# Keys by token of blocks 3 to 12: four turns of the activated keys and a product on VectorE, in place of eight turns of the finished keys and two copies on ScalarE

## What is computed

```
k = silu(x @ Wk)                                  # 16 heads of 8
k = concatenate([k * cos(theta*n), k * sin(theta*n)], -1)   # n: the token's number in its sequence
energy = (q @ k.T) * causal_mask                  # per head
out = energy @ v
```

## Time and profile before

| | us |
|---|---|
| median of 3 runs | 818.68 |
| lowest, highest | 814.37, 819.54 |
| the profiled execution, its time | 816.64 |
| its span, first to last instruction | 814.9 |

### The profile page before, as it was taken

How to read it: one execution, slowest core, us unless ns; L and a number is a source line. 1 busy time by engine, 2 the same in 40 slices (tenths; PEclk the granted TensorE clock), 3 DMA queues, 4 the chain that set the end, 5 groups by cost and what they waited for, 6 DMA issues and landing times.

```text
span 814.9 us, 27612 instructions
## 1 busy us (share of the span) xinstructions
PE 764.3 (94%) x10798; PEld 617.1 (76%) x10798; DVE 587.7 (72%) x1865; ACT 378.9 (46%) x826; POOL 441.6 (54%) x446
## 2 busy tenths in 40 slices
PE   5889999999999999999988899889999999999993
PEld 4666777777777777777776666779899998999883
DVE  7487898988889888898887899734544445443684
ACT  6434565746556465564653432223332233333583
POOL 6441344634446354453554665661877777876332
PEclk9999999999999999999999999999999999999998
DMA  4155334253442434434242322122554344443555
GB/s 149 45 177 178 102 93 109 66 125 74 101 104 75 120 77 102 103 77 116 63 113 66 80 68 84 40 72 93 105 99 86 42 96 99 72 56 43 134 139 148
DMA packets 73712, 77.18 MB, mean 95 GB/s; under 512 B 11955, under 2 KB 54762, under 8 KB 73584
## 3 DMA queue, kind: packets, MB, share of 16 engines
q1 hardware_dynamic: 56488, 59.15, 27.2%
q0 software_dynamic: 17024, 16.28, 11.2%
q10 hardware_dynamic: 72, 0.00, 0.0%
HBM read 23.99 MB, written 28.89 MB: 65 GB/s over the span
## 4 chain that ended last, share of the span: by engine, by line
PE 72%; DVE 17%; issue 6%; DMA 2%; POOL 2%; ACT 1%; DVEq 0%; POOLq 0%; ACTq 0%; SPq 0%
PE bank L1958 5%; PE bank L2540 4%; PE energy_and_gate_banks L2540 4%; PE bank L1960 4%; PE bank L1959 4%; PE energy_and_gate_banks L1958 4%; DVE EM L1348 3%; PE energy_banks L1958 3%; PE bank L1999 3%; PE energy_banks L1960 3%; PE energy_banks L1959 3%; PE energy_banks L2054 3%; PE energy_and_gate_banks L1960 3%; PE energy_and_gate_banks L1959 3%; PE energy_and_gate_banks L2090 3%
## 5 line engine op out<-in xcount | busy, mean ns | idle before, releaser
L707 POOL DMA_INDIRECT dispatched_rows<-x,slot x128 | 136.4, 1066 | 195.1 <-PE energy_banks L2054 98.8
L847 POOL DMA_INDIRECT summed_rows<-VP,goal_i x80 | 123.8, 1548 | 42.7 <-issue 22.7
L1224 ACT ACTIVATE sq<-energy_banks 128x512 f32<-128x512 f32 (+1 forms) x96 | 50.5, 527 | 120.2 <-PE energy_banks L1960 116.6
L933 ACT ACTIVATE hidden_rounded<-sf 128x512 fp32r<-128x512 f32 x88 | 55.3, 628 | 60.7 <-DVE sf L1378 60.7
L923 ACT ACTIVATE sf<-energy_and_gate_banks 128x512 f32<-128x512 f32 x88 | 52.4, 596 | 62.8 <-PE energy_and_gate_banks L1960 62.3
L1378 DVE TENSOR_TENSOR sf<-sf,bank 128x512 f32<-128x512 f32 x88 | 60.2, 684 | 15.6 <-PE bank L1960 14.5
L1348 DVE TENSOR_TENSOR EM<-energy_and_gate_banks,causal 128x512 f32<-128x512 f32 x64 | 43.9, 686 | 19.1 <-PE energy_banks L2079 13.1
L1958 PE MATMUL energy_and_gate_banks<-xgT_hi,ws_hi 128*128 128x512 f32 x108 | 51.8, 480 | 4.2 <-DVE EM L1348 2.8
L1958 PE MATMUL bank<-xgT_hi,ws_hi 128*128 128x512 f32 x108 | 46.0, 426 | 3.4 <-DVE sf L1378 1.9
L1830 DVE TENSOR_TENSOR he<-sq,bank 128x512 f32<-128x512 f32 (+1 forms) x48 | 28.7, 599 | 27.1 <-PE bank L1960 22.3
L1348 DVE TENSOR_TENSOR EM<-energy_banks,causal 128x512 f32<-128x512 f32 x64 | 43.4, 678 | 0.0
(11 more groups left out here) (271 smaller groups left out, 2266.0 us busy)
## 6 DMA issues: line engine op xcount, KB each, us to landing
QM<-QT SPq DMA_DIRECT2D x248, 32.0 KB
dispatched_rows<-empty POOLq DMA_DIRECT2D x8, 655.0 KB, 4.9
QM<-dispatched_rows SPq DMA_DIRECT2D x8, 655.0 KB, 6.0
QT<-sq SPq DMA_DIRECT2D x40, 128.0 KB
KT<-sq SPq DMA_DIRECT2D x40, 128.0 KB
VP<-QM SPq DMA_DIRECT2D x20, 256.0 KB
xin<-in_x SPq DMA_DIRECT2D x16, 256.0 KB, 4.0
QM<-summed_rows SPq DMA_DIRECT2D x16, 256.0 KB, 2.8
```

What stands on the lines that cost most here:

```text
L707: g.indirect_dma_start(out=xg_d, out_offset=bass.IndirectOffsetOnAxis(ap=slot[:, n % 2, j:j + 1], axis=0), in_=x1[:, n % 2, j % NC, :], in ...
L847: g.indirect_dma_start(out=sum_d, out_offset=bass.IndirectOffsetOnAxis(ap=goal_i[:, par, t:t + 1], axis=0), in_=ye[:, par, t, :], in_offse ...
L933: a.activation(hs_hi[:, f], sf[:, n % SF], ACT.Copy).then_inc(a_hh, 1)
```

## The change

- `keys_once_turned` on PE, right after `shared_pair(1)`: four 128x128 transposes of `sq[:, 1]`, the 128 activated key features, into PB[1]. `keys_turned` is no longer called in steps 2 to 11.
- `keys_by_token` moves from ACT to DVE, between `mask_state(5)` and `hidden_lo(1)`: two products of 128x512 that read 256 columns of PB[1] each (every element twice) and `table_T`, the angle table with tokens in partitions, and write `Kt`. `values_projected(1)` now waits for them, since it writes PB[1].
- `table_T` is made once: eight transposes of `table` into UB in steps 1 and 2 (`table_turned`, PE, after `input_turned`) and two copies on ACT (`table_by_token`). It lies in `x1t`, which the SP program fills from step 12 on.
- `input_turned` and `turn_x1` wait for the values and the gate (`a_v`, `a_th`), which are the last to read their banks, in place of `a_kt`; POOL's `dispatch` number 6 waits for the energies (`pe_E`) in place of the turned keys; ACT's Silu of the keys waits until the keys of the block before are turned.
- The token numbers are raised by a `tensor_tensor` with a tensor `two_blocks` [128, 4] that holds 1024, in place of the `tensor_scalar` with the number.

The same numbers are computed in both. The diff, cut to its core:

```diff
+        table_T = flat(x1t).rearrange("p (c n) -> p c n", c=NC)
...
# POOL
-                    need(gp, pe_kt, 2 * f + 2)
+                    need(gp, pe_E, 8 * b + 8)
                     dispatch(b - 1, (6,))
...
# ACT
+                    if i == 1 and projected_once(f - 1):
+                        need(act, pe_kt, 2 * f)
...
+                def table_by_token(i):
+                    need(act, pe_tab, i + 1)
+                    a.activation(table_T[:, 2 * i:2 * i + 2], UB[:].rearrange("p (c n) -> p c n", c=2), ACT.Copy).then_inc(a_tab, 1)
...
                     hidden_hi(b, 5)
-                    keys_by_token()
                     shared_silu(b, 6)
...
# DVE
-                v.tensor_scalar(x1[:, buf, :, D], x1[:, buf, :, D], 2.0 * S, None, ALU.add).then_inc(v_tok, 1)
+                if b == 1:
+                    dve.wait_ge(c_two, 1)
+                v.tensor_tensor(x1[:, buf, :, D], x1[:, buf, :, D], two_blocks[:], ALU.add).then_inc(v_tok, 1)
...
+                def keys_by_token():
+                    for i in (0, 1):
+                        need(dve, pe_kt, 2 * f + i + 1)
+                        need(dve, pe_S, NS * (f - 1))
+                        need(dve, a_tab, 2)
+                        by_feature = PB[1][:, 256 * i:256 * i + 256].unsqueeze(2).broadcast_to([P, 256, 2])
+                        v.tensor_tensor(Kt[:, fp, 2 * i:2 * i + 2].rearrange("p c (k t) -> p (c k) t", t=2), by_feature,
+                                        table_T[:, 2 * i:2 * i + 2].rearrange("p c (k t) -> p (c k) t", t=2), ALU.mult).then_inc(a_kt, 1)
...
                     mask_state(b, 5)
+                    keys_by_token()
                     hidden_lo(b, 1)
...
# PE
                 def input_turned(n=f):
-                    if n > 1:
+                    if projected_once(n - 1):
+                        need(pe, a_v, 4 * n - 2)
+                        need(pe, a_th, 2 * n - 1)
+                    elif n > 1:
                         need(pe, a_kt, 2 * n - 1)
...
                 def values_projected(i):
...
+                    if projected_once(f) and i == 1:
+                        need(pe, a_kt, 2 * f + 2)
...
+                def keys_once_turned():
+                    need(pe, a_silu, 4 * f + 4)
+                    need(pe, v_lg, f - 2)
+                    for c in range(NC):
+                        ins = t.transpose(PB[1][:, P * c:P * (c + 1)], sq[:, 1, P * c:P * (c + 1)], ident[:])
+                        if c % 2:
+                            ins.then_inc(pe_kt, 1)
...
                     shared_pair(1)
+                    keys_once_turned()
                     states_and_out(2)
...
                     energies_and_state(3)
-                    keys_turned()
                     positions(b)
```

More of the change, by code:

```diff
@@ L96, in build @@
         table = sb("table", [P, 2, S])
+        two_blocks = sb("two_blocks", [P, NC])
         rwt_s = sb("rwt_s", [P, E])
@@ L205, in build @@
         EB = [EB2[:, 0], EB2[:, 1], GB, UB]
-        ld_w = sem("weights_loaded"); ld_q = sem("wqk_loaded"); ld_g = sem("wv_g1_g2_loaded"); ld_t = sem("theta_loaded"); z_vp = sem("values_cleared"); z_qm = sem("q_by_head_cleared"); ld_x = sem("x_loaded"); c_pool = sem("pool_constants"); c_id = sem("identity")
+        ld_w = sem("weights_loaded"); ld_q = sem("wqk_loaded"); ld_g = sem("wv_g1_g2_loaded"); ld_t = sem("theta_loaded"); z_vp = sem("values_cleared"); z_qm = sem("q_by_head_cleared"); ld_x = sem("x_loaded"); c_pool = sem("pool_constants"); c_id = sem("identity"); c_two = sem("token_step_ready")
         c_dve = sem("dve_constants"); c_sin = sem("table_ready"); c_g = sem("g1g2_product"); a_wq = sem("wqk_hi_ready"); v_wq = sem("wqk_lo_ready"); v_ang = sem("angles_ready"); a_g = sem("g1g2_copied"); a_wvg = sem("wvg_hi_ready"); v_wvg = sem("wvg_lo_ready"); a_bf = sem("before_ready"); c_warm = sem("act_table_warm")
@@ L216, in build @@
         pe_kt = sem("k_by_token")
+        pe_tab = sem("table_turned"); a_tab = sem("table_by_token")
         pe_E = sem("energies")
@@ L484, in step @@
                     need(sp, v_x1, 4 * (b - 1))
+                    need(sp, a_kt, 2 * (DIRECT + 2) + 2)
                     sp.dma_start(sum_b[b - 2].rearrange("p (c d) -> p c d", c=NC), x1[:, par, :, 0:D]).then_inc(sp_x1b, 16)
@@ L641, in _ @@
             g.memset(expert[:], 0.0).then_inc(c_pool, 1)
+            g.memset(two_blocks[:], 2.0 * S).then_inc(c_two, 1)
             gp.wait_ge(ld_q, 16)
@@ L1011, in first_blocks @@
                         copy_out(b - 1, 3, 1 - par)
+                        table_by_token(0)
                     silu(f, fp, 0)
@@ L1046, in with_feed_forward @@
                         silu(f, fp, 0)
+                        table_by_token(1)
                         rows_turned()
@@ L2189, in values_projected, with table_turned @@
                     ins.then_inc(pe_vg, 1)
+                def table_turned(i):
+                    if i == 0:
+                        need(pe, a_xhi, 2)
+                    need(pe, a_tab, i)
+                    for c in (0, 1):
+                        for half in (0, 1):
+                            ins = t.transpose(UB[:, 256 * c + P * half:256 * c + P * half + P],
+                                              table[:, half, P * (2 * i + c):P * (2 * i + c + 1)], ident[:])
+                    ins.then_inc(pe_tab, 1)
+                def keys_once_turned():
[5 more added lines that the diff above has]
+                            ins.then_inc(pe_kt, 1)
                 def keys_turned():
@@ L2220, in first_blocks @@
                         input_turned()
+                        table_turned(0)
                     states_and_out(0)
@@ L2245, in with_feed_forward @@
                         input_turned()
+                        table_turned(1)
                         states_and_out(0)
@@ L2262, in with_feed_forward @@
                     project(f, 1)
+                    if b == 2:
+                        need(pe, a_tab, 2)
                     shared_up(0)
@@ L2372, in turn_x1 @@
                 need(pe, v_x1, 4 * (b - 1))
-                need(pe, a_kt, 2 * last(b) + 2)
+                if projected_once(last(b)):
+                    need(pe, a_v, 4 * last(b) + 4)
+                    need(pe, a_th, 2 * last(b) + 2)
+                else:
+                    need(pe, a_kt, 2 * last(b) + 2)
                 if DIRECT + 2 < b < B - 1:
```

## The result

| | before | after |
|---|---|---|
| median of 10 runs, us | 818.28 | 822.57 |
| lowest, highest | 812.58, 820.01 | 820.22, 827.18 |
| profiled execution: its time, its span | 816.64, 814.9 | 821.94, 820.2 |

The ratio is 1.0073, with a 95% interval of 1.0051 to 1.0094: slower by 0.7%, clear of noise and inside what was called "within 1%". The forecast was 825.0, which is 1.0077 of the 818.68 it started from. By the medians the kernel is 4.3 us slower, by the means of the ten runs (817.11 and 823.16) 6.0.

What follows compares the result with a forecast made beforehand. The prediction took PE and VectorE to bound stretches of each step in turn; only the products counted, 10 x 0.63 = +6.3 us on 818.68, giving 825.0 us. Its own range was 823.5 to 827.5, eight times in ten 817.5 to 829.0.

Steps and rivals of the forecast that it cites:

- What bounds: Chain through a step: PE to about 345 us, VectorE to mask(2), PE to energies 3, VectorE, then PE from 363.27.
- Rival A: PE's spared turns reach the end: 0.46 us less a step, 4.6 us in all, 814.1 us; chance 0.08.
- The turns removed: Eight turns on PE after energies 3, 0.93 us a step, beside mask(3) on VectorE: counted 0.
- The turns added: Four turns on PE after pair 1, 0.46 us against slacks of 0.66 and 0.49: counted 0, bound 0.1 a step.
- The products: Two new VectorE products of 128x512, taken at 0.60 us each, 1.20 a step; upper value 0.75 each.
- rival C: New products cost more than a mask's, 0.75 to 0.90 us each: 828.0 to 831.0 us; chance 0.18.
- Where they land: Products between mask_state(5) and hidden_lo(1): 1.20 us less 0.57 spare makes shared_hidden(3) and then PE 0.63 late a step.
- L1405: Raising token numbers at the head of the step: a possible 1.10 us gain on VectorE becomes idle time, counted 0.
- rival D: The new form of the token-number instruction waits as the old did; time as forecast, sharing the forecast's chance of 0.62.
- The table: Eight turns and two copies once, in steps 1 and 2 where PE is idle: counted 0, 0.9 us if uncovered.
- The sum: Ten steps at 0.63 us late each: +6.3 us, 825.0 us on the median.

Runs made afterwards that it cites:

- early_product: Changed kernel plus an extra 128x512 VectorE product behind rows_of_block_lo in steps 3 to 11, where VectorE waits for PE: 35.06 us a step, ratio to before 1.0071.
- third_product: Changed kernel plus a third product of the same shape between the two new ones on VectorE: 35.66 us a step, ratio to the kernel before 1.0133.
- old_turns_kept: Changed kernel with the eight old turns put back on PE between energies 3 and positions, read by nobody: 35.07 us a step, ratio to before 1.0074.
- split_products: Changed kernel with the second new product moved on VectorE to behind shared_hidden(4): 34.49 us a step, ratio to the kernel before 0.9996.
- bias_later: Changed kernel with POOL's input_and_bias of steps 4 to 11 moved behind pair_values and the first energies: 35.07 us a step, ratio to before 1.0069.
- tokens_later: Changed kernel with the raising of token numbers in steps 3 to 11 moved on VectorE behind rows_of_block_lo: 35.10 us a step, ratio to before 1.0068.

## Why the prediction was right

- *What bounds.* The chain's way through a step was read rightly: PE to 345, VectorE to mask(2), PE to energies 3, VectorE to the up of pair 7. early_product and third_product show that the same work on VectorE costs nothing in the first part and all of itself behind mask(2). Rival A, which had the kernel 4.6 us faster, fell with the result.
- *The turns removed* were counted at 0 for being beside mask(3). old_turns_kept: 0.02 us a step.
- *The turns added* were counted at 0 with a bound of 0.1. They take 0.44 on the chain (352.53), nearly the 0.46 counted. But the slack of 0.49 was read from the end of the last energies to the start of mask(2), as if VectorE could start at the very end of a matmul. It starts about 0.1 later: in the product of shared_hidden(0), step 10 of the kernel before, the up ends at 344.04 and the product starts at 344.14; at mask(2) of the changed kernel the last energies end at 356.42 and the mask starts at 356.55. So mask(2) starts 0.68 after shared_hidden(2) (355.87, 356.55), where it started 0.60 after it, and 0.08 comes through, within the bound. It is the term that was missed.
- *The products* were taken at 0.60, from the mask's product. L1549 takes 679 ns by its median (677 to 682) and the next starts 0.60 later. That each PSUM number is read twice costs nothing, and rival C falls. The larger fixed cost for a PSUM source that the Trainium skill gives ("VectorE: DVE Perf Modes", on the TRN2 errata) doesn't show here either: 679 ns, against 684 with both operands in SBUF.
- *Where they land.* 1.20 - 0.57 = 0.63 a step. From mask(2) to shared_hidden(3) it was 2.50 us (351.33, 353.83) and is 3.13 now (356.55, 359.68): 0.63. With the turns' 0.08 this makes 0.71, against 0.68 to 0.69 measured from step to step, so nothing is left for other causes, ScalarE's copies among them. split_products gives 0.56 back for moving one product out of the way.
- *L1405.* Its gain was counted at 0 for the right reason (bias_later), but the evidence on how it would turn out was read the wrong way. Against the rule of the Trainium skill ("SBUF — State Buffer", on its two separate sides) the prediction held that a hidden_lo had run beside POOL's L808 in 0.68. The rule held in the case that counts: the tensor form, with two operands in SBUF, took 1.25 us and ended with L699, as the other form had (rival D), and tokens_later shows a hidden_lo doing the same. The row taken as evidence was of a POOL instruction on 8 numbers a partition; L699 is on 512. The sum did not hang on it; a plan that counted on the 1.10 us would have failed.
- *The table.* 0 was right as far as the trace tells. Its turns lie in PE's idle time: the matmuls behind them had waited 0.95 and 1.38 us and wait 0.51 and 0.60 now, and they start no later (36.61 and 57.48 before). The start of step 3's down projection, 90.34 before and 90.69 after, says little, as it lies anywhere from 88.48 to 91.79 in the runs of the table above.

```profile
35.42 0.60 PE L2230 MATMUL bank<-ident,table 128*128 128x128 f32 x4
...
36.53 0.43 PE L2052 MATMUL energy_banks<-QT,SM 64*32 64x64 f32 x16 [0.51 <-issue]
...
57.27 0.43 PE L2052 MATMUL energy_banks<-QT,SM 64*32 64x64 f32 x16 [0.60 <-issue]
```

- *The sum.* Forecast +6.3. Nine steps give 9 x 0.69 = 6.2. At step 12's down projection the changed kernel is 6.5 us late (406.15, 399.62), and 5.3 at the end of the profiled executions; the ratio is worth 6.0. That the total comes so near is partly luck, as the part behind step 12 alone varies by 8.2 us between the runs. From that place to the end the programs do the same but for the form of the token numbers, and this part took 415.2 us before and 414.1 after; over all the runs above it lies between 411.5 and 419.7. The 1.2 us by which 5.3 falls short of 6.5 are within that scatter, whose cause was not looked into. The step times are the firmer measure for this reason.

## What to carry to other kernels

Before moving work to a less busy engine, follow the chain through one period and put a number on the slack at the exact place where the new instruction goes: here 0.57 us of slack decided over 1.20 us of work, and moving one of two instructions five places down took most of the loss away (0.56 of 0.68 a step). The same holds for what is removed: 0.93 us of the busiest engine was worth 0.02, since another engine ended later there. And a reordering that shortens one stretch lengthens another's: read the chain again after it, as the next one may be as late.

## What the runs showed of the hardware

- A VectorE instruction with two operands in SBUF waits for POOL's L699 (128x512, with operands in SBUF) when that is under way: 1.25 us in place of 0.16 for 128x4 numbers, with an end within 0.03 us of POOL's, and 1.8 in place of 0.68 for 128x512. In the profile this wait is a long duration of the waiting instruction; no idle time stands before it, and no releaser is named.
- The wait goes both ways. A product that had started 0.1 us before L699 (336.48 and 336.57 in the changed kernel) ran in its usual 0.68, and L699 took 1.73 there. In bias_later, beside products and masks that read one operand from PSUM, it takes 1.29, and they keep their 0.68 and 0.69:

```profile
341.28 1.29 POOL L699 TENSOR_TENSOR xb<-xin,bet 128x512 f32<-128x512 f32 x1 [1.25 <-PE energy_banks L2120]
```

- Beside POOL's 128x8 reciprocal root (L813, 1.67 us) a hidden_lo took 0.68 (335.88 in the changed kernel): that instruction held nobody. It is on 8 numbers a partition where L699 is on 512; whether this is the reason was not tested. Beside POOL's copies two hidden_lo took 1.57 for 1.28.
- A tensor_scalar and a tensor_tensor of 128x4 numbers waited alike (1.26, 1.25), and alone take 0.16 both.
- A VectorE product that reads each number of PSUM twice, through a step of 0, takes the time of a plain one: 679 ns for 512 results.
- At the two places read here VectorE starts 0.10 and 0.13 us after the end of the matmul that releases it (344.04 and 344.14, 356.42 and 356.55). The ends of matmuls are modelled in the profile, so this is to be taken off a slack that is read from such an end.
